# 21 of 24 later convolutions move from VectorE to TensorE, and the skip term from TensorE to ScalarE

## The chip, the cores and the metric

The kernel runs on one core of a Trainium2 chip. The metric is the device time of one execution in microseconds. Instructions are issued in program order on five engines, which wait for each other only through semaphores: TensorE (PE), VectorE (DVE), ScalarE (ACT), GpSimd (POOL) and SyncE (SP), which issues most of the transfers.

## The reference

For 2 x 1024 tokens with 512 features (all in float32) the reference computes a layer norm, a selective-scan block and a small top-2-of-8 mixture of experts, and joins them:

```
xn  = layernorm(x)
x, gate = split(xn @ W_in.T)                      # 1024 channels each
xc  = conv_b + sum_j conv_w[:, j] * xpad[:, j:j+L]   # 4 taps, causal, per channel
x   = silu(xc)
ts, B, C = rms(split(x @ W_x.T))                  # 32, 16, 16
dt  = softplus(ts @ W_dt.T + b_dt)
state = state * exp(dt * A) + (dt * x) * B        # 16 states per channel, over time
y   = (sum_n state * C + x * D) * silu(gate)
s   = y @ W_out.T
g   = silu(mixture of 2 of 8 experts on xn)
out = x_in + s * g
```

## The kernel before

The 2048 tokens are cut into four chunks c of 512 (two per batch row), and the 1024 channels into eight blocks t of 128. A tile n = 8c + t is one block of one chunk. Its 16 states are worked in four quads: quad m = 4n + q has four recurrences (r = 0 to 3) over 512 time steps, each with 32 channels x 4 states on the partitions. "Low" is r = 0, 1, "high" is r = 2, 3.

For each quad: POOL multiplies `rep` (dt * x, spread over partitions by a transfer through DRAM) with B into one of four ring buffers of `drive` (`drives`, L567). ACT writes the decays exp(dt * A) into the four banks of `sc_ps` (`decays`, L799), two banks at a time, each after DVE or POOL is done with them. DVE runs the recurrences (`scans`, L1174) and multiplies by C (`products`, L1184); in most tiles POOL multiplies the low half of three or four quads instead (`low_products`, L580). PE sums over the states into `y_ps` (`sums`, L1434), after a start value that `skip` puts there: a matmul of x with a diagonal matrix of D (L1428), whose diagonal ACT writes (`diagonal`, L852). At the end DVE multiplies `y_ps` by the gate (`gate_tile`, L1201), a quad later than the last scans of the tile, behind the first quad of the next.

During chunk c the eight blocks of x for chunk c + 1 are made, each in four steps. PE projects into the bank `x_ps` (`next_x`, `project_x`, L1329). ACT copies it, with three columns of the chunk before, to `x_pad` and writes the first tap with its bias back over `x_ps` (`copy_x`, L703 to L710). DVE adds the other three taps, one instruction each, the last into `xy` (`convolve`, L1113). ACT takes the SiLU (`silu_x`, L715). "Early" blocks (1, 3, 5, 7) are in tiles t = 3, 4, 5, 6 ahead of the high scans of quad 4n + 1, "late" blocks (0, 2, 4, 6) in tiles t = 2, 3, 4, 5 behind the high products of quad 4n + 2. There is one `x_ps` bank and one `x_pad`, so each block waits for the one before it.

In the same tile dt of tile n + 2 is made: a matmul (`step_sizes`), ACT's Abs, Exp and Ln (`softplus`), and three instructions and a product on DVE (L1153 to L1157, L1149). In nine tiles (`pe_log`) PE adds the four parts by matmuls with the identity instead (`add_log`, L1378 to L1381), one of them the maximum, which ACT writes to `t_r`. Two "slots" of 128 gathered tokens go through an expert per tile in the middle of each row: POOL issues the gather, PE turns the rows (`turn_slot`), ACT copies them (`copy_slot_T`), PE multiplies (`expert`), ACT copies the result out (`copy_slot_y`). SP loads the expert's 1024 KB for each, and the weights of the next projections.

The order on each engine is written out by hand in one loop over n per engine. No planner changes it.

Of the kernel before, what the change touches and what calls it, by code (L numbers as in the profile page):

```python
# [50 lines left out]
LATE_X = {2: 0, 3: 2, 4: 4, 5: 6}  # L51

# [47 lines left out]
def scan_moe(nc, x, wx_in, wg_in, wdt_in, wxp, wring, gate_w, means, a_log, conv_w, conv_b, d_skip,  # L100
             token_ids, route_consts, bc_dram, rep_rows, xn_rows, xnT_rows, order, slot_rows, s_rows, out):
    with ExitStack() as ctx:
# [47 lines left out]

        w_gate = t_r[:, 0:HK * CH].rearrange("p (k e) -> p k e", k=HK)
# [120 lines left out]
        diag_ok, skip_mm = sem("diag_ok"), sem("skip_mm")  # L272
        x_mm, x_ev = sem("x_mm"), sem("x_ev")
        pad_ok, tap_ok, halo_ok = sem("pad_ok"), sem("tap_ok"), sem("halo_ok")
# [32 lines left out]

        def drives_done(eng, count):
            eng.wait_ge(drive_ok, count)
# [6 lines left out]
        def _(sp):  # L316
# [125 lines left out]
            for n in range(TILES):  # L442
                c, t = divmod(n, NT)
                b, even = c // PER_ROW, c % PER_ROW == 0
                first_slot, second_slot = slots_at(c, t)
                if n == 2:
                    for half in range(2):
                        sp.dma_start(w_out[:, HK * half:HK * (half + 1), :], wring[E + half]).then_inc(s_wo, 16)
                chunk_end = t == NT - 1 and c < NCH - 1
                if not even and t == NT - 2:  # L450
                    load_kept(c - 1)
                    load_residual(c - 1)
                if c == NCH - 1 and t == NT - 2:
# [24 lines left out]
                if c and t == 1 and c + 1 < NCH:  # L478
                    load_xnT(c + 1)
                if first_slot is not None:  # L480
                    load_expert(b, first_slot + 2)
                if chunk_end:
                    spread_b(c + 1, NQ - 1)
                    spread_c(c + 1, 1)
                if late_x(c, t) is not None:
                    load_w_x(NT * (c + 1) + late_x(c, t) + 1)
                if early_x(c, t) == NT - 1 and c + 2 < NCH:
                    load_w_x(NT * (c + 2))
                if second_slot is not None:
                    load_expert(b, second_slot + 2)  # L490
                if not even and t == NT - 1:
# [187 lines left out]
        def _(act):  # L679
# [16 lines left out]
            def copy_x(j):  # L696
                c, t = divmod(j, NT)
                kept = j - 2 if j < NT else j
                if kept > 0:
                    act.wait_ge(conv_ok, kept)  # L700
                    act.wait_ge(halo_ok, kept)
# [10 lines left out]
            def silu_x(j):  # L712
                c, t = divmod(j, NT)
                act.wait_ge(conv_ok, j + 1)
                act.activation(xy[:, c % 2, t, :], xy[:, c % 2, t, :], ACT.Silu).then_inc(x_ok, 1)  # L715
# [24 lines left out]
            def exponent(k):  # L740
# [6 lines left out]
                if pe_log(k):  # L747
                    act.activation(t_r[:, :], dt_ps[:, :], ACT.Relu).then_inc(relu_ok, 1)
# [100 lines left out]
            def diagonal(n):  # L849
                if n:  # L850
                    act.wait_ge(skip_mm, n)
                act.activation(diag[:, :], ident[:, :], ACT.Copy, scale=dsk[:, n % NT:n % NT + 1]).then_inc(diag_ok, 1)  # L852
# [53 lines left out]
            for n in range(TILES):  # L906
# [19 lines left out]
                diagonal(n)  # L926
# [11 lines left out]
                decays(m + 1, 1)  # L938
                copy_slot_T(b, first_slot)
# [41 lines left out]
        def _(dve):  # L981
# [311 lines left out]
        def _(pe):  # L1293
# [39 lines left out]
            def next_x(j):  # L1333
                c, t = divmod(j, NT)
                pe.wait_ge(s_wx, 16 * (j - NT + 1))
                pe.wait_ge(conv_ok, j)
# [10 lines left out]
                project_x(j, lambda h: w_x[:, h, :])  # L1347

# [23 lines left out]
            def add_log(k):  # L1372
# [5 lines left out]
                pe.matmul(dt_ps[:, :], ident[:, :], t_e[:, :], start=True, stop=False)  # L1378
                pe.matmul(dt_ps[:, :], ident[:, :], t_w[:, :], start=False, stop=False)
                pe.matmul(dt_ps[:, :], ident[:, :], t_l[:, :], start=False, stop=False)  # L1380
                pe.matmul(dt_ps[:, :], ident[:, :], t_r[:, :], start=False, stop=True).then_inc(log_mm, 1)  # L1381
# [41 lines left out]
            def skip(n):  # L1423
                c, t = divmod(n, NT)
                pe.wait_ge(diag_ok, n + 1)
                if n:
                    pe.wait_ge(gated, n)
                pe.matmul(y_ps[:, :], diag[:, :], xy[:, c % 2, t, :], start=True, stop=False).then_inc(skip_mm, 1)  # L1428

            def sums(m):  # L1430
                low_done(pe, m)
                pe.wait_ge(high_ok, m + 1)
                for r in range(NR):
                    last = pe.matmul(y_ps[CH * r:CH * (r + 1), :], stack[:, :], drive[:, m % RING, r, :],  # L1434
                                     start=False, stop=(m % NQ == NQ - 1))
# [65 lines left out]
            for n in range(TILES):  # L1501
# [14 lines left out]
                turn_slot(b, first_slot)  # L1516
                skip(n)
# [4 lines left out]
                if rms_tile:  # L1522
                    pe.wait_ge(conv_ok, NT * (c + 2))
# [19 lines left out]
                expert(b, second_slot)  # L1543
# [4 lines left out]
                sums(m + 2)  # L1548
                if not even and t in (0, 1):
# [81 lines left out]
```

## Time and profile before

| | us |
|---|---|
| median of three timed runs | 1090.31 (1086.61 to 1090.49) |
| span of the profiled execution, first to last instruction | 1086.8 |
| busy in the span: DVE, POOL, PE, ACT | 1022.8, 926.3, 872.1, 733.8 |
| convolutions of chunks 1 to 3 on DVE | 24 |
| matmuls of `skip` on PE (records, two for each) | 64 |

For the profiled execution only the span is given; it is 3.5 us under the median and 0.2 over the fastest timed run. Where a row has the count of matmul records, two records are one float32 matmul here. The profile's idle time of an engine is put down to the one that released it last.

### The profile page before, as it was taken

To read this page: it belongs to the slowest core of one execution; us is meant where nothing else is said; L and a number is where in the kernel's file an instruction comes from. 1 tells how busy PE (TensorE), PEld (TensorE's weight loads), DVE (VectorE), ACT (ScalarE), POOL (GpSimd) and SP (SyncE) were. 2 spreads that over 40 slices of the span, in tenths; PEclk is the share of its full clock that TensorE was granted. 3 is DMA by queue.
4 is the path that set the end of the run, shared out by engine and by line. 5 is a ranking of instruction groups with operands and counts; after the bars stand their busy time and mean duration, and the time that the engine had idled before them with its cause. 6 is when DMAs were issued, how large, how long until landed. Compare 5 with 4: busy or idle time off the path is not lost.

```text
span 1086.8 us, 10255 instructions
## 1 busy us (share of the span) xinstructions
PE 872.1 (80%) x2774; PEld 323.8 (30%) x2774; DVE 1022.8 (94%) x1044; ACT 733.8 (68%) x1285; POOL 926.3 (85%) x365
## 2 busy tenths in 40 slices
PE   9944569798889998988656778989788997778576
PEld 5321123233223433333112223333223342223122
DVE  6779999999999999999999999899999999999998
ACT  3655567787787667766775667778767566676574
POOL 0629899999989889989889989798998978998995
PEclk9976788999989999999967879999999999799789
DMA  9355586556476665666743554766548566565714
GB/s 331 120 161 199 107 268 232 212 198 232 167 274 240 232 238 207 170 182 210 204 164 122 185 181 152 274 242 227 190 165 287 188 224 232 184 225 182 280 33 151
DMA packets 78089, 219.26 MB, mean 202 GB/s; under 512 B 15824, under 2 KB 17232, under 8 KB 71376
## 3 DMA queue, kind: packets, MB, share of 16 engines
q1 hardware_dynamic: 58096, 166.67, 44.7%
q10 hardware_dynamic: 12672, 31.46, 7.8%
q0 software_dynamic: 7264, 20.47, 6.9%
q8 instruction: 23, 0.38, 0.1%
q14 instruction: 34, 0.28, 0.1%
HBM read 176.85 MB, written 41.72 MB: 201 GB/s over the span
## 4 chain that ended last, share of the span: by engine, by line
DVE 36%; PE 22%; POOL 15%; issue 12%; DMA 9%; ACT 4%; SPq 2%; DVEq 0%; ACTq 0%; POOLq 0%
DVE sc_ps L1174 16%; POOL drive L567 10%; DVE drive L1174 6%; PE x_ps L1466 6%; DMA rep<-rep_rows 5%; DVE drive L1184 3%; PE f_ps L1419 3%; POOL drive L580 3%; PE y_ps L1434 3%; DMA x_slot<-xn_rows,slot_tok 2%; PE dt_ps L1394 2%; DVE x_ps L1113 2%; PE x_ps L1329 1%; PE x_ps L1351 1%; SPq L382 1%
## 5 line engine op out<-in xcount | busy, mean ns | idle before, releaser
L567 POOL TENSOR_TENSOR drive<-rep,b_all 128x2048 f32<-128x2048 f32 x127 | 575.8, 4538 | 44.1 <-DMA rep<-rep_rows 40.7
L799 ACT ACTIVATE sc_ps<-rep,a_neg 128x512 f32<-128x512 f32 x512 | 332.0, 681 | 86.2 <-DVE drive L1184 57.3
L1434 PE MATMUL y_ps<-drive,stack 128*32 128x512 f32 x1024 | 156.1, 687 | 89.7 <-DVE drive L1184 62.8
L1184 DVE TENSOR_TENSOR drive<-sc_ps,c_all 128x1024 f32<-128x1024 f32 x177 | 216.8, 1225 | 5.9
L1174 DVE TENSOR_TENSOR_SCAN sc_ps<-sc_ps,state,drive 128x512 f32<-128x512 f32 x178 | 218.4, 1273 | 3.8 <-ACT sc_ps L799 3.2
L1174 DVE TENSOR_TENSOR_SCAN sc_ps<-sc_ps,drive 128x512 f32<-128x512 f32 x176 | 205.3, 1212 | 5.5 <-ACT sc_ps L799 4.4
L580 POOL TENSOR_TENSOR drive<-drive,c_all 128x1024 f32<-128x1024 f32 x79 | 186.4, 2360 | 6.1 <-ACT state L778 6.1
L1419 PE MATMUL f_ps<-w_ring,xT_slot 128*128 128x512 f32 x368 | 176.5, 624 | 12.1 <-ACT xT_slot L811 12.1
L1394 PE MATMUL dt_ps<-xnT,w_g 128*128 128x512 f32 x232 | 117.8, 655 | 20.5 <-ACT dtu L766 20.4
L1419 PEld LDWEIGHTS f_ps<-w_ring,xT_slot 128*128 128x128 f32 x368 | 71.5, 201 | 118.3 <-issue 118.0
L1174 DVE TENSOR_TENSOR_SCAN drive<-sc_ps,state,drive 128x512 f32<-128x512 f32 x78 | 95.5, 1266 | 2.8 <-ACT sc_ps L799 2.8
L1174 DVE TENSOR_TENSOR_SCAN drive<-sc_ps,drive 128x512 f32<-128x512 f32 x80 | 93.1, 1205 | 0.0
L1329 PE MATMUL x_ps<-xnT,w_x 128*128 128x512 f32 x192 | 89.7, 611 | 2.7 <-DMA w_x<-wx_in 2.7
L1466 PE MATMUL x_ps<-w_out,xy 128*128 128x512 f32 x176 | 84.8, 629 | 0.0
L1434 PEld LDWEIGHTS y_ps<-drive,stack 128*32 128x32 f32 x1024 | 21.9, 114 | 183.8 <-issue 142.3
L1394 PEld LDWEIGHTS dt_ps<-xnT,w_g 128*128 128x128 f32 x232 | 46.0, 209 | 97.1 <-issue 97.1
L778 ACT ACTIVATE state<-sc_ps 128x2 f32<-128x2 f32 x88 | 14.9, 169 | 71.0 <-DVE drive L1184 70.3
L536 POOL DMA_INDIRECT x_slot<-xn_rows,slot_tok x46 | 45.5, 989 | 20.0 <-PE f_ps L1408 13.7
L1370 PE MATMUL dt_ps<-dt_in,w_dt 128*128 128x512 f32 x64 | 44.4, 783 | 14.2 <-DVE dt_in L1231 13.0
L1408 PE MATMUL f_ps<-ident,x_slot 128*128 128x128 f32 x184 | 29.4, 284 | 31.9 <-DMA x_slot<-xn_rows,slot_tok 26.8
L1428 PE MATMUL y_ps<-xy,diag 128*128 128x512 f32 x64 | 35.8, 643 | 20.7 <-DVE xy L1201 20.7
L1329 PEld LDWEIGHTS x_ps<-xnT,w_x 128*128 128x128 f32 x192 | 35.5, 193 | 56.3 <-issue 52.7
(200 smaller groups left out, 1093.8 us busy)
## 6 DMA issues: line engine op xcount, KB each, us to landing
rep<-rep_rows SPq DMA_DIRECT2D x128, 512.0 KB, 6.7
w_ring<-wring SPq DMA_DIRECT2D x46, 1024.0 KB, 5.6
rep_rows<-dtu ACTq DMA_DIRECT2D x32, 512.0 KB, 3.3
slot_rows<-y_slot ACTq DMA_DIRECT2D x46, 256.0 KB
w_g<-wg_in SPq DMA_DIRECT2D x32, 256.0 KB, 2.7
w_x<-wx_in SPq DMA_DIRECT2D x24, 256.0 KB
xn_rows<-rep SPq DMA_DIRECT2D x16, 256.0 KB, 2.2
b_all<-bc_rows SPq DMA_DIRECT2D x16, 256.0 KB, 4.3
```

Of the source, the lines that this page charges most:

```text
L536: pool.indirect_dma_start(x_slot[:, :], None, xn_rows[:, :], bass.IndirectOffsetOnAxis(ap=slot_tok[:, m:m + 1], axis=0)).then_inc(s_gx, 16)
L567: pool.tensor_tensor(drive[:, m % RING, :, :], rep[:, n % 2, :, 1, :], b_all[:, q:q + 1, :].broadcast_to([P, NR, TC]), ALU.mult).then_inc( ...
L580: pool.tensor_tensor(drive[:, m % RING, 0:2, :], drive[:, m % RING, 0:2, :], c_all[:, q:q + 1, :].broadcast_to([P, 2, TC]), ALU.mult).then ...
L799: act.activation(sc[:, r, :], rep[:, n % 2, r, 0, :], ACT.Exp, scale=a_neg[:, lo:lo + 1]).then_inc(decay_ok, 1)
L1174: dve.tensor_tensor_scan(to, sc[:, r, :], drive[:, m % RING, r, :], state[:, lo:lo + 1] if follows else 0.0, ALU.mult, ALU.add).then_inc(s ...
L1184: dve.tensor_tensor(drive[:, m % RING, 2 * h:2 * h + 2, :], sc[:, 2 * h:2 * h + 2, :], c_all[:, q:q + 1, :].broadcast_to([P, 2, TC]), ALU. ...
L1329: last = pe.matmul(x_bank(j), w(h), xnT[:, c % 2, h, :], start=(h == 0), stop=(h == HK - 1))
L1370: pe.matmul(dt_ps[:, :], w_dt[:, t, :], dt_in[:, :], start=True, stop=True).then_inc(dt_mm, 1)
L1394: mm = pe.matmul(gate_bank(c, t)[:, :], w_g[:, h, :], xnT[:, c % 2, h, :], start=(h == 0), stop=(h == HK - 1))
L1419: last = pe.matmul(f_ps[:, :], xT_slot[:, h, :], w_ring[:, j % 2, h, :], start=(h == 0), stop=(h == HK - 1))
L1434: last = pe.matmul(y_ps[CH * r:CH * (r + 1), :], stack[:, :], drive[:, m % RING, r, :], start=False, stop=(m % NQ == NQ - 1))
L1466: last = pe.matmul(bank, xy[:, c % 2, t, P * i:P * (i + 1)], w_out[:, t, :], start=(t == 0), stop=(t == NT - 1))
```

## The change

- In chunks 1 to 3 the blocks 0 to 6 get their last three taps on PE: three matmuls with diagonal matrices (`add_taps`), added to the first tap that ACT has written in `x_ps`. Block 7 and chunk 0 stay on DVE. The matrices (192 KB for a block) are loaded by SP (`load_taps`) into `t_r`.
- For early blocks ACT's SiLU reads `x_ps`. For late blocks ACT copies `x_ps` to `xy` first (`take_x`), behind the softplus, and the SiLU follows in the next tile as before.
- On PE the early taps stand before `skip`; `sums(m + 1)` moves ahead of the late projection; the late taps and the second expert stand behind `sums(m + 2)`. On ACT the late `copy_x` moves behind the decays of the low half of quad m + 3.
- From tile 1 on, `skip` is an ACT instruction that writes x * D into `y_ps`, and the sums are added to it. It stands behind the high decays of quad m + 1. The diagonal is left for tile 0.
- In `pe_log` tiles ACT writes the maximum over `dt_ps` in place, and PE adds three parts.

```diff
+PE_TAPS = (0, 1, 2, 3, 4, 5, 6)
+def pe_taps(j):
+    return j >= NT and j % NT in PE_TAPS
+def late_taps(j):
+    return pe_taps(j) and j % NT in LATE_X.values()
...
+        def x_bank_free(eng, j):
+            if late_taps(j - 1):
+                eng.wait_ge(x_took, took(j))
+            elif pe_taps(j - 1):
+                eng.wait_ge(x_ok, j)
+            else:
+                eng.wait_ge(conv_ok, dve_convs(j))
...
+            def load_taps(j):
+                if j is None or not pe_taps(j):
+                    return
+                if pe_convs(j):
+                    sp.wait_ge(taps_mm, pe_convs(j))
+                else:
+                    sp.wait_ge(lgT_mm, 1)
+                sp.dma_start(taps, taps_in[j % NT]).then_inc(s_tap, 16)
...
             def silu_x(j):
...
+                elif pe_taps(j):
+                    act.wait_ge(taps_mm, pe_convs(j + 1))
+                    xy_free(act, c)
+                    rows = x_ps[:, :]
...
+            def take_x(j):
+                if not late_taps(j):
+                    return
+                c, t = divmod(j, NT)
+                act.wait_ge(taps_mm, pe_convs(j + 1))
+                xy_free(act, c)
+                act.copy(xy[:, c % 2, t, :], x_ps[:, :]).then_inc(x_took, 1)
...
-                    act.activation(t_r[:, :], dt_ps[:, :], ACT.Relu).then_inc(relu_ok, 1)
+                    act.activation(dt_ps[:, :], dt_ps[:, :], ACT.Relu).then_inc(relu_ok, 1)
...
+            def skip(n):
+                if n == 0:
+                    return
+                c, t = divmod(n, NT)
+                act.wait_ge(gated, n)
+                act.activation(y_ps[:, :], xy[:, c % 2, t, :], ACT.Copy, scale=dsk[:, t:t + 1]).then_inc(skip_ok, 1)
...
                 decays(m + 1, 1)
+                skip(n)
                 copy_slot_T(b, first_slot)
...
                 copy_slot_y(b, first_slot)
+                store_slot(b, first_slot)
+                decays(m + 3, 0)
                 if late is not None:
                     copy_x(NT * (c + 1) + late)
-                store_slot(b, first_slot)
-                decays(m + 3, 0)
                 copy_slot_T(b, second_slot)
...
+                if late is not None:
+                    take_x(NT * (c + 1) + late)
...
+            def add_taps(j):
+                if not pe_taps(j):
+                    return
+                pe.wait_ge(s_tap, 16 * pe_convs(j + 1))
+                pe.wait_ge(tap_ok, j + 1)
+                for k in range(1, K):
+                    last = pe.matmul(x_ps[:, :], taps[:, k - 1, :], x_pad[:, k:k + TC], start=False, stop=(k == K - 1),
+                                     skip_group_check=True)
+                last.then_inc(taps_mm, 1)
...
                 turn_slot(b, first_slot)
+                if early_x(c, t) is not None:
+                    add_taps(NT * (c + 1) + early_x(c, t))
                 skip(n)
...
+                sums(m + 1)
                 if late is not None:
                     next_x(NT * (c + 1) + late)
                 turn_slot(b, second_slot)
-                sums(m + 1)
...
-                expert(b, second_slot)
+                if late is None:
+                    expert(b, second_slot)
...
                 sums(m + 2)
+                if late is not None:
+                    add_taps(NT * (c + 1) + late)
+                    expert(b, second_slot)
```

## Rows read from the trace of the kernel before

**Rows 1.** The page's busy line: us, share of the span, instructions.
```profile
PE 872.1 (80%) x2774; PEld 323.8 (30%) x2774; DVE 1022.8 (94%) x1044; ACT 733.8 (68%) x1285; POOL 926.3 (85%) x365
```

**Rows 2.** Windows of tiles 4 and 27: busy us by engine, granted clock, transfers.
```profile
212.00:241.00 29.00, 25.69 (x83) 9.40 (x83) 28.72 (x29) 23.96 (x47) 26.52 (x10) 1.00 0.60 207
930.00:959.00 29.00, 21.06 (x70) 7.38 (x68) 28.29 (x27) 18.65 (x29) 28.64 (x10) 0.88 0.61 205
```

**Rows 3.** Groups of instructions, whole span: busy us, mean ns of one, idle before.
```profile
L799 ACT ACTIVATE sc_ps<-rep,a_neg 128x512 f32<-128x512 f32 x512 | 332.0, 681 | 86.2 <-DVE drive L1184 57.3 <-DVE drive L1174 10.6 <-DMA rep<-rep_rows 6.4
L1329 PE MATMUL x_ps<-xnT,w_x 128*128 128x512 f32 x192 | 89.7, 611 | 2.7 <-DMA w_x<-wx_in 2.7
L1113 DVE SCALAR_TENSOR_TENSOR x_ps<-x_pad,cw,x_ps 128x512 f32<-128x512 f32 x54 | 40.4, 749 | 3.1 <-ACT x_ps L708 2.0 <-DVE moe L993 0.2
L1428 PE MATMUL y_ps<-xy,diag 128*128 128x512 f32 x64 | 35.8, 643 | 20.7 <-DVE xy L1201 20.7
L708 ACT ACTIVATE x_ps<-x_pad,cb,cw 128x512 f32<-128x512 f32 x27 | 21.1, 782 | 2.5
L705 ACT COPY x_pad<-x_ps 128x512 f32<-128x512 f32 x27 | 15.5, 575 | 16.6 <-PE x_ps L1329 16.6
L852 ACT ACTIVATE diag<-ident,dsk 128x128 f32<-128x128 f32 x32 | 13.0, 407 | 0.0
```

**Rows 4.** DVE in order of time, tiles 2 and 4: start, us, [idle before].
```profile
167.30 2.35 DVE L1174 TENSOR_TENSOR_SCAN sc_ps<-sc_ps,drive 128x512 f32<-128x512 f32 x2 [0.99 <-ACT sc_ps L799]
...
215.73 1.52 DVE L1113 SCALAR_TENSOR_TENSOR x_ps<-x_pad,cw,x_ps 128x512 f32<-128x512 f32 x2
...
217.95 2.34 DVE L1174 TENSOR_TENSOR_SCAN sc_ps<-sc_ps,drive 128x512 f32<-128x512 f32 x2
...
223.71 2.32 DVE L1174 TENSOR_TENSOR_SCAN sc_ps<-sc_ps,drive 128x512 f32<-128x512 f32 x2
...
235.19 2.33 DVE L1174 TENSOR_TENSOR_SCAN drive<-sc_ps,drive 128x512 f32<-128x512 f32 x2
```

**Rows 5.** ACT in order of time, tile 4.
```profile
211.73 0.78 ACT L708 ACTIVATE x_ps<-x_pad,cb,cw 128x512 f32<-128x512 f32 x1
...
215.84 0.20 ACT L778 ACTIVATE state<-drive 128x2 f32<-128x2 f32 x1 [0.82 <-DVE drive L1174]
...
221.84 1.30 ACT L799 ACTIVATE sc_ps<-rep,a_neg 128x512 f32<-128x512 f32 x2
...
232.17 1.30 ACT L799 ACTIVATE sc_ps<-rep,a_neg 128x512 f32<-128x512 f32 x2
```

**Rows 6.** PE in order of time, tiles 2 and 4.
```profile
164.73 1.12 PE L1408 MATMUL f_ps<-ident,x_slot 128*128 128x128 f32 x4 [5.84 <-DMA x_slot<-xn_rows,slot_tok]
...
215.17 3.67 PE L1419 MATMUL f_ps<-w_ring,xT_slot 128*128 128x512 f32 x8 [0.36 <-ACT xT_slot L811]
...
239.18 1.07 PE L1434 MATMUL y_ps<-drive,stack 128*32 128x512 f32 x8
```

**Rows 7.** The page's transfers: count, KB each, median us to landing.
```profile
w_ring<-wring SPq DMA_DIRECT2D x46, 1024.0 KB, 5.6
```

**Rows 8.** POOL in order of time, tile 4.
```profile
222.87 4.54 POOL L567 TENSOR_TENSOR drive<-rep,b_all 128x2048 f32<-128x2048 f32 x1 [2.12 <-DMA rep<-rep_rows]
```

**Rows 9.** DVE in order of time: the gates that end tiles 1, 5, 9, 13, 25, 29.
```profile
148.31 0.68 DVE L1201 TENSOR_TENSOR xy<-y_ps,gate 128x512 f32<-128x512 f32 x1
...
273.64 0.68 DVE L1201 TENSOR_TENSOR xy<-y_ps,gate 128x512 f32<-128x512 f32 x1
...
390.85 0.69 DVE L1201 TENSOR_TENSOR xy<-y_ps,gate 128x512 f32<-128x512 f32 x1 [0.56 <-PE y_ps L1434]
...
519.84 0.68 DVE L1201 TENSOR_TENSOR xy<-y_ps,gate 128x512 f32<-128x512 f32 x1
...
900.50 0.69 DVE L1201 TENSOR_TENSOR xy<-y_ps,gate 128x512 f32<-128x512 f32 x1 [0.99 <-PE y_ps L1434]
...
1015.92 0.68 DVE L1201 TENSOR_TENSOR xy<-y_ps,gate 128x512 f32<-128x512 f32 x1
```

More of the change, by code:

```diff
@@ L51, with pe_convs, dve_convs, took @@
 LATE_X = {2: 0, 3: 2, 4: 4, 5: 6}
+PE_TAPS = (0, 1, 2, 3, 4, 5, 6)
+def pe_taps(j):
+    return j >= NT and j % NT in PE_TAPS
+def pe_convs(k):
+    return sum(pe_taps(j) for j in range(k))
+def dve_convs(k):
+    return k - pe_convs(k)
+def late_taps(j):
+    return pe_taps(j) and j % NT in LATE_X.values()
+def took(k):
+    return sum(late_taps(j) for j in range(k))
 def act_turns(k):
@@ L149, in scan_moe @@
         slot_tok = sb("slot_tok", BATCH * SLOTS, dtype=I32)
+        taps = t_r[:, 0:(K - 1) * P].rearrange("p (k e) -> p k e", k=K - 1)
         w_gate = t_r[:, 0:HK * CH].rearrange("p (k e) -> p k e", k=HK)
@@ L481, in _ @@
                     load_expert(b, first_slot + 2)
+                if late_x(c, t) is not None and t > 2:
+                    load_taps(NT * (c + 1) + late_x(c, t))
                 if chunk_end:
@@ L490, in _ @@
                     load_expert(b, second_slot + 2)
+                if t == 1 and c < NCH - 1:
+                    load_taps(NT * (c + 1) + late_x(c, t + 1))
+                if early_x(c, t + 1) is not None:
+                    load_taps(NT * (c + 1) + early_x(c, t + 1))
                 if not even and t == NT - 1:
@@ L699, in copy_x @@
                 if kept > 0:
-                    act.wait_ge(conv_ok, kept)
+                    if pe_taps(kept - 1):
+                        act.wait_ge(taps_mm, pe_convs(kept))
+                    else:
+                        act.wait_ge(conv_ok, dve_convs(kept))
                     act.wait_ge(halo_ok, kept)
@@ L713, in silu_x @@
                 c, t = divmod(j, NT)
-                act.wait_ge(conv_ok, j + 1)
-                act.activation(xy[:, c % 2, t, :], xy[:, c % 2, t, :], ACT.Silu).then_inc(x_ok, 1)
+                if late_taps(j):
+                    act.wait_ge(x_took, took(j + 1))
+                    rows = xy[:, c % 2, t, :]
+                elif pe_taps(j):
+                    act.wait_ge(taps_mm, pe_convs(j + 1))
+                    xy_free(act, c)
+                    rows = x_ps[:, :]
+                else:
+                    act.wait_ge(conv_ok, dve_convs(j + 1))
+                    rows = xy[:, c % 2, t, :]
+                act.activation(xy[:, c % 2, t, :], rows, ACT.Silu).then_inc(x_ok, 1)
+            def take_x(j):
[5 more added lines that the diff above has]
+                act.copy(xy[:, c % 2, t, :], x_ps[:, :]).then_inc(x_took, 1)
             act.wait_ge(ln_v, 1)
@@ L1377, in add_log @@
                 pe.wait_ge(relu_ok, pe_logs(k + 1))
[L1378 to L1381, printed above, removed]
+                pe.matmul(dt_ps[:, :], ident[:, :], t_e[:, :], start=False, stop=False, skip_group_check=True)
+                pe.matmul(dt_ps[:, :], ident[:, :], t_w[:, :], start=False, stop=False, skip_group_check=True)
+                pe.matmul(dt_ps[:, :], ident[:, :], t_l[:, :], start=False, stop=True, skip_group_check=True).then_inc(log_mm, 1)
             def gate_in(n):
@@ L1423, in skip @@
             def skip(n):
-                c, t = divmod(n, NT)
-                pe.wait_ge(diag_ok, n + 1)
                 if n:
-                    pe.wait_ge(gated, n)
-                pe.matmul(y_ps[:, :], diag[:, :], xy[:, c % 2, t, :], start=True, stop=False).then_inc(skip_mm, 1)
+                    pe.wait_ge(skip_ok, n)
+                    return
+                pe.wait_ge(diag_ok, 1)
+                pe.matmul(y_ps[:, :], diag[:, :], xy[:, 0, 0, :], start=True, stop=False)
             def sums(m):
@@ L1434, in sums @@
                     last = pe.matmul(y_ps[CH * r:CH * (r + 1), :], stack[:, :], drive[:, m % RING, r, :],
-                                     start=False, stop=(m % NQ == NQ - 1))
+                                     start=False, stop=(m % NQ == NQ - 1), skip_group_check=m >= NQ)
                 last.then_inc(sum_ok, 1)
@@ L1590 @@
     gate_w[:, :E] = v["gate_w"]
+    taps = np.zeros((NT, P, K - 1, P), f)
+    for k in range(1, K):
+        taps[:, np.arange(P), k - 1, np.arange(P)] = v["conv_w"].reshape(NT, P, K)[:, :, k]
     consts = np.ones((P, CONSTS), f)
@@ L1607 @@
         "gate_w": gate_w.reshape(HK, P, CH).transpose(1, 0, 2),
+        "taps_in": taps,
         "means": mean_w,
```

33 lines of the change are left out of this document (19 added, 14 removed).

## The prediction

> **What bounds the kernel now.** I read the page's busy line first: VectorE (DVE) is busy 94% of the span, GpSimd (POOL) 85%, TensorE (PE) 80%, ScalarE (ACT) 68% [rows 1]. The start-up is in these shares. Then I read windows of single tiles, for how close the others are: in the 29 us of tile 4 DVE works 28.72, POOL 26.52, PE 25.69, ACT 23.96 [rows 2]. So DVE sets the pace, with three engines close behind. All four are coupled: ACT writes the decays into the four banks of `sc_ps` only when DVE has left them, DVE scans only behind them, and PE must finish `sums(m)` before POOL refills the ring. A saving on DVE is therefore worth what the next engine lets through.
>
> **What is removed from DVE.** 21 convolutions of three instructions. One takes 749 ns [rows 3]; on the clock the three stand between the scan pair that ends at 215.73 and the next at 217.95, so 2.22 us each [rows 4]. 21 x 2.22 = 46.6 us, all of it on the engine that sets the pace. That is the largest possible gain: a span of 1040.2.
>
> **What it is replaced by.** Chunks 1 to 3 take nine of these convolutions as early ones (before the scans of the tile's second quad, t = 3, 4, 5) and twelve as late ones (t = 2 to 5). I walk through tile 4, which has one of each, and move every piece by what changed ahead of it.
>
> *Early.* After low(m+1) DVE goes straight to the scans at 215.73. The next half quads follow without a gap, so DVE stands at the scans of (m+2, high) at 223.71 - 2.22 = 221.49 [rows 4]. ACT writes those decays at 221.84, one of them takes 0.68, so the first is there at 222.52 [rows 3, 5]. It can't come sooner: ahead of it on ACT lie two table loads, two SiLUs and the gate's SiLU without a gap. The skip activation of ScalarE is new ahead of this, but ACT stood idle 0.82 us at 215.84 for DVE [rows 5]. The skip is priced between the decay's 681 ns (ScalarE, SBUF to PSUM) and the 782 of the scaled first tap (the same way) [rows 3]; I take 0.68, and 0.82 covers both ends. Without that cover it would delay the decays by 0.7 per tile. Stall 1.03, net gain 2.22 - 1.03 = 1.2 per early convolution: 9 x 1.2 = 10.8.
>
> *Late.* DVE comes to low(m+4) at 235.19 now [rows 4]; less 1.2 and 2.22 it would be 231.8. ACT starts those decays at 232.17 [rows 5], gets `take_x` in front (a 128x512 copy out of PSUM, 575 ns by the copy to x_pad [rows 3]), so 232.75, and the first is ready at 233.4. Stall 1.6, net 0.6. This holds where softplus n+2 ends on PE. Where it ends on DVE, three instructions of about 0.7 and the product stand before low(m+4) and cover it, and only some 0.2 is lost before the decays of (m+3, high): net 2.0. Of the nine late ones in t = 3 to 5, five are of the first kind (n = 4, 11, 12, 13, 20), four of the second: 5 x 0.6 + 4 x 2.0 = 11.0. At t = 2 (three tiles) another thing sets the pace: in tile 2 PE waits 5.84 us for the gathered rows at 164.73 [rows 6], ACT's `copy_slot_T` stands behind it, and DVE waits 0.99 for the decays behind that [rows 4]. There a convolution less is only a longer wait, between 0 and 2.2; I take 0.7, since only tile 2's row shows it: 2.1.
>
> *PE.* A matmul pair of `project_x` costs 89.7/96 = 0.93 us of busy time, one skip pair 35.8/32 = 1.1 [rows 3]. A tile with two tapped projections gets 6 x 0.93 = 5.6 more and 1.1 less: 25.69 + 4.5 = 30.2 busy in tile 4 [rows 2], more than the 27.4 that this tile would take by the sums above. Busy records overlap, so this isn't a hard bound, but PE has no slack left in t = 3 to 5. The early taps cost little: they need ACT's first tap, written at 211.73 + 0.78 = 212.5 [rows 5], and until the expert's matmuls start at 215.17 PE has only the skip and idle time [rows 6]; 3 x 0.93 ends at about 215.3, and the skip that went to ACT comes at the same time. So `sums(m)` moves by 0.6 at most. The late taps and the second expert go behind `sums(m+2)`, and with the next projection push `sums(m+3)` from 239.18 [rows 6] to about 239.3, while DVE has come forward by 1.8. In tile 5 PE then starts as late as before, its projection for the late convolution ends later relative to DVE, and `copy_x` on ACT (in order ahead of the decays of (m+3, high)) waits for it. My walk through tile 5 gives 2.2 saved where the terms above give 3.2; bounds are 0 and a whole late saving of 2. I charge 1.0 in t = 4 and t = 5 of chunks 0 and 2, half in chunk 1 (longer tiles): -5.
>
> *The rest.* `add_log` loses one matmul (nine times) and the maximum goes in place: no DVE instruction changes, and the later steps of t wait for ACT's Ln, so 0 (bounds: 0.93 us gained or lost in each of nine tiles, if it stood on the path). 31 diagonals of 407 ns are replaced by 31 skips: +0.27 us each on ACT [rows 3], hidden by its waits; `skip` waits for `gated`, which DVE gives one instruction after the product that releases the decays ahead of it, so it waits for nothing new; behind it stand `copy_slot_T`, and through that PE's expert and `sums(m)`. The new loads are 21 x 192 KB on SP's queue. The tightest is the late one, issued behind an expert load of 1024 KB, which itself waits for the expert matmuls (end 215.17 + 3.67 = 218.8 [rows 6]). With 5.6 us to landing [rows 7] and 192 KB more at the same rate (1.1) it is there at 225.5; PE wants it at about 226.9, when the late first tap ends, which now follows the decays of (m+3, low). Cost 0, with 1 us as the upper bound in nine tiles. SP's waits for `taps_mm` follow waits for the expert's matmuls that now end later than the taps, so they hold up nothing more, and the rep loads keep their release, `gate_in`'s last matmul.
>
> **Sum.** 10.8 + 11.0 + 2.1 - 5 = 18.9, say 19 to 20. POOL must allow it: it starts drive(4n+4) at 222.87, after 2.12 idle for the rep rows [rows 8], and is done 7.8 us before DVE wants it at 235.19 [rows 4]; 5 us stay. The span is 1086.8, and the median of the timed runs 1090.31 is 3.5 above it, which I carry along: 1090.3 - 20 = **1070**.
>
> By the Trainium skill (Perfetto Trace Analysis, Identifying the Most-Contended Engine) TensorE's matmul busy share is no measure of how near it is to its limit, since matmuls are pipelined; then the 30.2 above would be no bound and the 5 us charged to PE would fall away, which would give 1065. Rows 2 can't settle it, since they are of the busy kind; the other sentences keep the charge.
>
> **Rivals.**
> (a) *The gap closes further.* Chunk 3 has no convolutions: tiles 26 to 29 run from 900.50 to 1015.92, 28.9 us each, against 31.3 in tiles 2 to 5 (148.31 to 273.64) and 32.2 in tiles 10 to 13 (390.85 to 519.84) [rows 9]. If the tapped tiles came down to 28.9: 4 x 2.4 + 4 x 3.3 and chunk 2 like chunk 0, so 10 + 13 + 10 = 33, or 1057. For it: the late `copy_x` goes behind the decays of (m+3, low) on ACT, which takes pressure from one of its three tight places. Against: chunk 3 has no projection, no first tap and no state to keep on ACT (18.65 of 29 busy against 23.96), and even so POOL is at 28.64 of 29 there [rows 2], so this is about the floor that POOL sets. The whole 46.6 would give 1044; the same skill section tells to work on the most-occupied engine, which would be DVE. Chance 0.25 for (a), of which 0.04 for the whole.
> (b) *PE becomes the bound, slower.* The place is `next_x`(late) in t = 3 to 5, held up on PE by its new wait for `silu_x` of the early tile, and by taps; ACT stands in `copy_x`, DVE waits for decays. If PE needs its 30.2 busy us and keeps the 3.3 of idle time it has in tile 4 (29 - 25.69) [rows 2], a tile takes 33.5 against the 31.3 of tiles 2 to 5 [rows 9]: 9 x 2.2 = 20 lost, 1110. It decides as soon as PE's idle time in such a tile stays above 31.3 - 30.2 = 1.1 us. Against it: most of that idle time is just where the early taps go. Chance 0.11.
> (c) *Nothing moves.* The stalls at (m+2, high) and low(m+4) grow by all that is taken away, because ACT's sequence is full, and taps or gathers arrive late: 1090. For it: ACT's 0.58 and PE's 4.5 more in each tapped tile, and tile 2's wait. Against: t = 3 and t = 5 have the cover of DVE's three softplus steps. Chance 0.09.
>
> **How the numbers follow.** Forecast 0.55 (its own range 1062 to 1080), (a) 0.25, (b) 0.11, (c) 0.09. Half a per cent is 5.5 us, what a measurement of this kernel can tell: faster is forecast and (a), 0.80; same 0.09; slower 0.11. The range reaches down to between (a) and the whole, 1050, and up to (c), 1090.
>
> **What would show it.** Right: DVE's busy time falls by about 47 us while its idle time grows by about 27 (46.6 - 20), with new waits `sc_ps` scan <- ACT decays in t = 3 to 5, after (m+2, high) and at low(m+4) of tiles 4, 12 and 20; PE's busy time is up by some 16 us (21 x 2.8 less 31 x 1.1 and 9 x 0.93) and PE's idle before the expert's matmuls in tile 4 shrinks; POOL's durations unchanged. The PE step is wrong if the scans never wait for `copy_x`. Wrong altogether if DVE's idle time grows by over 40 us, or if tiles 6, 7 and those of chunk 3, which have no tapped convolution, get longer: then the skip on ACT isn't hidden.

## The result, and the profile after

The changed kernel takes 1143.91 us (median; 1141.73 to 1146.49), the kernel before 1089.35 on the same chip: a ratio of 1.050, 95% interval 1.0475 to 1.0524. It is slower by 55 us where 20 us of gain were forecast, and outside the range. The profiled execution has a span of 1141.6, 54.8 more than before.

The page's busy line of the changed kernel:
```profile
PE 898.6 (79%) x2820; PEld 338.1 (30%) x2820; DVE 980.9 (86%) x981; ACT 747.8 (66%) x1297; POOL 925.9 (81%) x365
```
Against [rows 1] DVE has lost 41.9 us of busy time, as intended, and idles 160.7 instead of 64.0: 96.7 more. Nobody else has much more to do (PE 26.5, ACT 14.0, POOL nothing). So this is waiting, and the waits say for what (who waited for whom: us, times, longest):
```profile
PE y_ps L1524 <- POOL drive L634: 85.3, 39, 6.8
DVE sc_ps L1255 <- ACT sc_ps L873: 62.3, 31, 5.1
...
POOL x_slot L590 <- PE f_ps L1498: 49.0, 16, 5.5
ACT x_pad L762 <- PE x_ps L1410: 48.4, 20, 6.0
ACT xT_slot L885 <- PE f_ps L1498: 45.1, 24, 4.4
...
ACT xy L789 <- PE x_ps L1436: 38.0, 11, 7.5
...
DVE drive L1255 <- ACT sc_ps L873: 34.4, 13, 5.6
```
PE's wait in `sums` for POOL's low product was 26.9 us before (15 times, 5.3 at the longest):
```profile
PE y_ps L1434 <- POOL drive L580: 26.9, 15, 5.3
```

The time from gate to gate by tile, worked out from the starts of `gate_tile`, shows where it is lost (us):

| tiles | before | after |
|---|---|---|
| t = 2 to 5 of chunks 0 to 2 (12 tiles) | 380.2 | 428.0 |
| the other tiles 1 to 23 (11) | 339.8 | 344.0 |
| chunk 3 (8) | 232.4 | 236.0 |

All but 8 us of it lies in the tapped tiles. Tile 4 went from 28.6 to 36.7. Its window, against the first of [rows 2] (DVE 28.72 of 29):
```profile
224.00:261.00 37.00, 33.35 (x108) 13.13 (x100) 24.52 (x23) 25.75 (x51) 28.59 (x11) 0.95 0.58 209
```
DVE stops three times for decays and once for dt, where [rows 4] have no such stop in tile 4 (DVE in order of time):
```profile
236.04 2.35 DVE L1255 TENSOR_TENSOR_SCAN sc_ps<-sc_ps,drive 128x512 f32<-128x512 f32 x2 [2.54 <-ACT sc_ps L873]
...
244.63 2.35 DVE L1255 TENSOR_TENSOR_SCAN sc_ps<-sc_ps,drive 128x512 f32<-128x512 f32 x2 [2.74 <-ACT sc_ps L873]
...
252.57 2.34 DVE L1255 TENSOR_TENSOR_SCAN drive<-sc_ps,drive 128x512 f32<-128x512 f32 x2 [4.33 <-ACT sc_ps L873]
257.06 0.69 DVE L1230 TENSOR_TENSOR dtu<-dt_ps,xy 128x512 f32<-128x512 f32 x1 [2.16 <-PE dt_ps L1471]
```
PE in the same tile. Before, the last sums of this tile at 239.18 [rows 6] had no wait, nor had the three ahead of them; now two of the sums wait for POOL:
```profile
237.01 1.07 PE L1524 MATMUL y_ps<-drive,stack 128*32 128x512 f32 x8 [1.18 <-POOL drive L634]
238.01 3.70 PE L1410 MATMUL x_ps<-xnT,w_x 128*128 128x512 f32 x8
...
245.48 1.07 PE L1524 MATMUL y_ps<-drive,stack 128*32 128x512 f32 x8 [2.48 <-POOL drive L634]
246.47 4.54 PE L1436 MATMUL x_ps<-x_pad,t_r 128*128 128x512 f32 x6
250.85 3.59 PE L1509 MATMUL f_ps<-w_ring,xT_slot 128*128 128x512 f32 x8
254.28 1.02 PE L1469 MATMUL dt_ps<-t_e,ident 128*128 128x512 f32 x2
```
And ACT, with the two copies that wait for PE and have the decays behind them:
```profile
241.74 0.58 ACT L762 COPY x_pad<-x_ps 128x512 f32<-128x512 f32 x1 [2.54 <-PE x_ps L1410]
...
251.05 0.58 ACT L789 COPY xy<-x_ps 128x512 f32<-128x512 f32 x1 [2.60 <-PE x_ps L1436]
```
Read together (the experiments below test it): POOL finishes a low product late, PE stands in the sum over it, the projection, the taps, the expert and the logarithm stand behind that sum, ACT stands in a copy for them, DVE in a scan for ACT. It closes to a loop on POOL, which issues the next gather only after PE has turned the rows (POOL in order of time):
```profile
229.10 0.99 POOL L590 DMA_INDIRECT x_slot<-xn_rows,slot_tok  x1 [4.62 <-PE f_ps L1498]
```

### The profile page after: what moved, and what is told of

The parts are those of the page before. It is cut to its first block, busy times and chain, and to the rows that moved or that the text cites. A ratio compares the mean times of both kernels' runs of the same rounds, so it can differ in the third digit from the quotient of the medians.

```text
span 1141.6 us, 10307 instructions
## 1 busy us (share of the span) xinstructions
PE 898.6 (79%) x2820; PEld 338.1 (30%) x2820; DVE 980.9 (86%) x981; ACT 747.8 (66%) x1297; POOL 925.9 (81%) x365
## 4 chain that ended last, share of the span: by engine, by line
PE 36%; POOL 20%; DMA 18%; DVE 15%; issue 5%; SPq 4%; ACT 2%; DVEq 0%; POOLq 0%; ACTq 0%
DMA rep<-rep_rows 13%; POOL drive L621 12%; DVE sc_ps L1255 7%; PE f_ps L1509 6%; PE dt_ps L1484 6%; PE x_ps L1556 5%; PE y_ps L1524 5%; POOL drive L634 4%; PE x_ps L1436 4%; PE x_ps L1410 4%; SPq L430 3%; DMA rep_rows<-dtu 2%; DVE drive L1265 2%; DMA slot_rows<-y_slot 1%; PE x_ps L1442 1%
## 5 line engine op out<-in xcount | busy, mean ns | idle before, releaser
L1524 PE MATMUL y_ps<-drive,stack 128*32 128x512 f32 x1024 | 160.2, 703 | 161.4 <-POOL drive L634 85.3
L1509 PE MATMUL f_ps<-w_ring,xT_slot 128*128 128x512 f32 x368 | 174.2, 618 | 18.4 <-ACT xT_slot L885 18.4
L1484 PE MATMUL dt_ps<-xnT,w_g 128*128 128x512 f32 x232 | 120.1, 666 | 20.9 <-ACT dtu L840 18.9
L1410 PE MATMUL x_ps<-xnT,w_x 128*128 128x512 f32 x192 | 92.0, 624 | 0.0
L1556 PE MATMUL x_ps<-w_out,xy 128*128 128x512 f32 x176 | 85.3, 632 | 0.0
L1484 PEld LDWEIGHTS dt_ps<-xnT,w_g 128*128 128x128 f32 x232 | 46.6, 212 | 97.3 <-issue 97.3
L1436 PE MATMUL x_ps<-x_pad,t_r 128*128 128x512 f32 x126 | 68.7, 687 | 0.0
L885 ACT COPY xT_slot<-f_ps 128x512 f32<-128x512 f32 x46 | 26.6, 578 | 45.4 <-PE f_ps L1498 45.1
L1461 PE MATMUL dt_ps<-dt_in,w_dt 128*128 128x512 f32 x64 | 40.4, 718 | 14.2 <-DVE dt_in L1312 13.0
L1556 PEld LDWEIGHTS x_ps<-w_out,xy 128*128 128x128 f32 x176 | 33.7, 200 | 50.3 <-issue 49.7
```

What stands on the lines that cost most here:

```text
L1410: last = pe.matmul(x_bank(j), w(h), xnT[:, c % 2, h, :], start=(h == 0), stop=(h == HK - 1))
L1436: last = pe.matmul(x_ps[:, :], taps[:, k - 1, :], x_pad[:, k:k + TC], start=False, stop=(k == K - 1), skip_group_check=True)
L1484: mm = pe.matmul(gate_bank(c, t)[:, :], w_g[:, h, :], xnT[:, c % 2, h, :], start=(h == 0), stop=(h == HK - 1))
L1509: last = pe.matmul(f_ps[:, :], xT_slot[:, h, :], w_ring[:, j % 2, h, :], start=(h == 0), stop=(h == HK - 1))
L1556: last = pe.matmul(bank, xy[:, c % 2, t, P * i:P * (i + 1)], w_out[:, t, :], start=(t == 0), stop=(t == NT - 1))
```

## The experiments

Every ratio is to runs of the kernel before on the same chip, whose median went from 1087.95 to 1090.79; "median, ratio [95% interval]". Two kernels leave two of the three tap matmuls out.

**First: is it the taps?** Four versions of the changed kernel.

No block tapped:
```diff
-PE_TAPS = (0, 1, 2, 3, 4, 5, 6)
+PE_TAPS = ()
```


> No block is tapped on TensorE (PE_TAPS is empty): all 24 convolutions are back on VectorE, while the skip on ScalarE, the maximum in place and the new order of the sums, of the late projection, of copy_x and of the second expert stay. Theory W (TensorE's work sets the length of a tapped tile): 1085 to 1090, since PE has 43 us less work than before. Theory C (the late taps stand behind the third sums and take_x ahead of the decays): also 1085 to 1092. Theory S (the skip on ScalarE and the new order cost the time, not the taps): 1120 to 1144.

Measured: 1136.33, 1.040 [1.033, 1.048]. Theories W and C are both out as the cause of the loss: with 24 convolutions on DVE and none on PE, 46 of the 55 us are still lost (S had 1120 to 1144). Something else in the change costs it.

Only the early blocks (`PE_TAPS = (1, 3, 5)`):

> Only the nine early blocks (1, 3, 5) are tapped on TensorE; the twelve late ones are back on VectorE, so take_x is gone. Theory W: a loss in proportion to TensorE's added work, 9 of 21 of it, so about 1089 + 23 = 1112. Theory C: the early taps fill idle time and save VectorE about 1 us each, 1080 to 1090.

Measured: 1132.13, 1.040 [1.034, 1.046]. In neither range.

Only the late blocks (`PE_TAPS = (0, 2, 4, 6)`):

> Only the twelve late blocks (0, 2, 4, 6) are tapped on TensorE; the nine early ones are on VectorE. Theory W: 12 of 21 of the loss, about 1120. Theory C: nearly all of the loss, 1135 to 1145.

Measured: 1138.65, 1.044 [1.037, 1.051]. Inside C's range, but without meaning once the first is known.

All blocks, one matmul instead of three:
```diff
-                for k in range(1, K):
+                for k in range(K - 1, K):
```


> All 21 blocks as in the changed kernel, but TensorE multiplies only the last tap of each and leaves out the two others: 42 matmuls of 0.86 us less, every wait and every other instruction stays. Theory W: 36 us less, about 1108. Theory C: the late taps end 1.7 us sooner and the wait of take_x shrinks by that in twelve tiles, 20 us at most, 1122 to 1135; the wait for the third sums stays.

Measured: 1123.56, 1.030 [1.024, 1.035]. By the medians some 20 us for 36 us of matmuls: in C's range and far from W's, but C was already out as the cause.

**Second: the order on PE.** In the kernel without taps DVE waited 8.7 us for a late first tap in tile 2, that for `next_x`, and that stood behind `sums(m + 1)`. So the kernel *before* got this one edit, and nothing else:
```diff
+                sums(m + 1)
                 if late is not None:
                     next_x(NT * (c + 1) + late)
                 turn_slot(b, second_slot)
-                sums(m + 1)
```


> The kernel before with one edit: on TensorE sums(m + 1) moves ahead of the late projection and the second slot's transposes. Theory O (this order alone costs the time: PE stands in sums(m + 1) for POOL's low product, next_x and copy_x stand behind it, and the late first tap comes late): 1115 to 1140, with VectorE waiting for the late convolution. Rival E (what costs is the second expert behind sums(m + 2), or the skip on ScalarE): 1086 to 1093.

Measured: 1141.92, 1.050 [1.047, 1.052], 2 us above O's range. One moved call with no instruction added loses 52 us, about as much as the whole change. PE and then DVE in tile 2:
```profile
163.61 1.93 PE L1434 MATMUL y_ps<-drive,stack 128*32 128x512 f32 x8 [8.30 <-POOL drive L580]
165.47 5.11 PE L1329 MATMUL x_ps<-xnT,w_x 128*128 128x512 f32 x8
```
```profile
172.11 1.55 DVE L1113 SCALAR_TENSOR_TENSOR x_ps<-x_pad,cw,x_ps 128x512 f32<-128x512 f32 x2 [11.51 <-ACT x_ps L708]
```
PE waits 8.30 us for a product that POOL reaches only after a drive and a gather. The projection that stood ahead of these sums in program order filled such time; now, behind them, it comes 10 us later than in the kernel before (155.19 there, by the same view), it runs partly at half clock (5.11 us for what takes 3.70), and DVE waits 11.51. Over the whole kernel DVE's wait for a first tap grew from 2.0 us to
```profile
DVE x_ps L1113 <- ACT x_ps L708: 50.3, 13, 11.5
```
and the profiled span by 44.3: the late first taps account for the loss.

The same move taken out of the changed kernel, in three versions (no taps, all, early only):

> The changed kernel without taps on TensorE (all 24 convolutions on VectorE), with sums(m + 1) back behind the late projection and the transposes; skip on ScalarE, maximum in place, copy_x behind the decays, second expert behind sums(m + 2) stay. Theory O: 1080 to 1095, the 45 us of the kernel without taps are gone. Rival E: stays at 1115 to 1137.

> The changed kernel with all 21 blocks tapped on TensorE and sums(m + 1) back behind the late projection and the transposes. Theory O with room on PE: 1070 to 1085, the gain that was forecast. Rival W (TensorE's work, some 32 us per tapped tile, is a second bound under the order's): 1095 to 1125. Rival E: no change, 1135 to 1144.

> As the last, but only the nine early blocks are tapped on TensorE. Theory O: 1075 to 1085 (nine early savings of 1.2 us each). Rival W: 1090 to 1105, since the tapped tiles t = 3 to 5 have 2.6 us more for PE each. Rival E: 1115 to 1132.

Measured: 1120.20, 1.026 [1.022, 1.031]; 1150.17, 1.054 [1.048, 1.059]; 1117.49, 1.028 [1.023, 1.032]. The first and the last lie in E's ranges, the one with all taps above all three. Theory O holds for the edit alone and falls as the only cause: with all taps this move alone gives nothing back (1.054 against 1.050). Without taps, 16 us came back, not 45, and DVE now waited 3.0 to 8.5 us for `dt_ps <- PE` in six tiles: 4, 11, 12, 13, 18, 20, the late tiles whose logarithm is on PE.

**Third: the second expert.** Again the kernel *before* with one edit:
```diff
-                expert(b, second_slot)
+                if late is None:
+                    expert(b, second_slot)
...
                 sums(m + 2)
+                if late is not None:
+                    expert(b, second_slot)
```


> The kernel before with one edit: in the tiles with a late block the second expert stands behind sums(m + 2) on TensorE. Theory Q (PE stands in the sum for POOL's low product and the expert and the logarithm's matmuls behind it come late): 1105 to 1125, with VectorE waiting for dt_ps in tiles 4, 11, 12, 13, 18, 20. Rival (it costs only together with the skip on ScalarE): 1088 to 1095.

Measured: 1121.45, 1.030 [1.027, 1.034], in Q's range. PE and then DVE in tile 4:
```profile
236.20 1.93 PE L1434 MATMUL y_ps<-drive,stack 128*32 128x512 f32 x8 [5.66 <-POOL drive L580]
238.06 5.67 PE L1419 MATMUL f_ps<-w_ring,xT_slot 128*128 128x512 f32 x8
```
```profile
247.20 0.69 DVE L1149 TENSOR_TENSOR dtu<-dt_ps,xy 128x512 f32<-128x512 f32 x1 [5.63 <-PE dt_ps L1381]
```
DVE waits for `dt_ps` like this in tiles 4, 11, 12, 13, 18 and 20, as forecast: 4.7 to 6.5 us each, 33.0 together, and the loss is 33.

Then the changed kernel with both moves undone:
```diff
-                sums(m + 1)
                 if late is not None:
                     next_x(NT * (c + 1) + late)
                 turn_slot(b, second_slot)
+                sums(m + 1)
...
-                if late is None:
-                    expert(b, second_slot)
+                expert(b, second_slot)
...
                 sums(m + 2)
                 if late is not None:
                     add_taps(NT * (c + 1) + late)
-                    expert(b, second_slot)
```
without taps, with all, with the early ones only, and with all but the late taps ahead of the third sums:

> No taps on TensorE, and both of PE's moves undone: sums(m + 1) behind the late projection and the transposes, the second expert ahead of sums(m + 2). What stays of the change is the skip on ScalarE, the maximum in place and copy_x behind the decays. Theory Q (PE, in program order, stands in a sum for POOL's low product, and what was moved behind it is late; each of the two moves alone is enough to cost 30 to 50 us): 1083 to 1093. Rival S (the skip on ScalarE costs): stays near 1110 to 1120.

> All 21 blocks tapped on TensorE with both moves of PE undone; the late taps stand behind sums(m + 2), take_x waits for them. Theory Q: the late taps are the third thing behind a sum that waits for POOL, with take_x and the decays of the next tile behind them, so 1110 to 1140. Rival W (PE's work alone): 1095 to 1110, whatever the place of the taps.

> Both moves of PE undone and only the nine early blocks tapped on TensorE; the twelve late ones are on VectorE. Theory Q: the early taps lie in PE's idle time: 1073 to 1086, faster than before. Rival W: 1095 to 1105.

The last one, against the one with all taps:
```diff
+                if late is not None:
+                    add_taps(NT * (c + 1) + late)
                 sums(m + 2)
-                if late is not None:
-                    add_taps(NT * (c + 1) + late)
```


> As the last, but the late taps stand ahead of sums(m + 2), behind the second expert. Theory Q: nothing of the late block stands behind a sum that waits for POOL: 1070 to 1095. Rival W: the same as the last kernel, within 5 us.

Measured: no taps 1097.28, 1.0075 [1.005, 1.010]; all, behind the third sums, 1102.26, 1.010 [1.004, 1.016]; early only 1099.52, 1.010 [1.006, 1.015]; all, late ones ahead, 1086.50, 0.998 [0.994, 1.001]. 39 of the 46 us without taps are back. The late taps' place is worth 16 us (1102.26 to 1086.50), the same in kind. Q's ranges held only for the last one. No taps came out 4 us above its range, and the other two fell between 1095 and 1110, where rival W had them: Q had the cost of the late taps behind the sum too high and the early taps' gain too high. W in turn is out by the last one, which has all of PE's work and is 16 us faster. These four ran on one chip, so the taps themselves can be priced: from no taps to all taps in their best place here 11 us, and for the early nine alone nothing (1097.28 to 1099.52, intervals overlap). PE's wait for POOL over these kernels (in order: only the sums moved; only the expert moved; both undone without taps; the last one):
```profile
PE y_ps L1434 <- POOL drive L580: 53.0, 18, 8.3
```
```profile
PE y_ps L1434 <- POOL drive L580: 83.3, 22, 7.2
```
```profile
PE y_ps L1524 <- POOL drive L634: 25.5, 14, 4.9
```
```profile
PE y_ps L1524 <- POOL drive L634: 24.3, 16, 5.2
```
Over all kernels it is 19 to 33 us in those of 1103 us or less and 53 to 98 in those of 1117 or more. The size doesn't order the losses (53.0 goes with 1142, 83.3 with 1121): what counts is what stands behind the sum.

**Fourth: why then no gain?** With the late taps ahead of the third sums, DVE stood 3.52 us in tile 4 for the decays of (m + 4, low). ACT shows why:
```profile
236.91 0.59 ACT L789 COPY xy<-x_ps 128x512 f32<-128x512 f32 x1 [1.78 <-PE x_ps L1436]
237.39 0.21 ACT L852 ACTIVATE state<-drive 128x2 f32<-128x2 f32 x1
237.63 1.30 ACT L873 ACTIVATE sc_ps<-rep,a_neg 128x512 f32<-128x512 f32 x2
```
Three single edits to that kernel. `take_x` behind the decays:
```diff
-                if late is not None:
-                    take_x(NT * (c + 1) + late)
                 decays(m + 4, 0)
+                if late is not None:
+                    take_x(NT * (c + 1) + late)
```


> The kernel with both moves undone and the late taps ahead of sums(m + 2), with one more edit: on ScalarE take_x stands behind the decays of (m + 4, low), not ahead of them. If the 3.5 us that VectorE waits at low(m + 4) in tiles 4, 11, 13 and 20 are take_x's wait for the taps: 1068 to 1080. If the SiLU block at (m + 2, high) and PE's work are what is left: 1082 to 1090.

Measured: 1082.30, 0.995 [0.993, 0.997]. The wait in tile 4 fell to 1.14, but the next one, for `dt_ps`, took 2.30. The kernel is faster than before by a measurable half per cent, and in the second range, not the first. What this edit gave by itself (4 us by the medians, on another chip, with overlapping intervals) isn't clear of noise.

The late `copy_x` in its old place, ahead of the decays of (m + 3, low):

> The same kernel with the late taps ahead of sums(m + 2), take_x as in the changed kernel, and the late copy_x back ahead of the decays of (m + 3, low). If ScalarE's late first tap is what the taps wait for, they and take_x end about 1.3 us sooner: 1075 to 1085. If nothing waits there: 1084 to 1089. If the decays of (m + 3, low) become late: 1090 to 1100.

Measured: 1095.73, 1.009 [1.006, 1.012], in the third range. The new place is worth 9 us by the medians and 12 by the ratios: a part of the change that helps.

The skip back on PE:

> The same kernel with the skip back on TensorE (diagonal by ScalarE, start matmul behind the gate). If the skip on ScalarE is what leaves 7 us in the kernel without taps: 1075 to 1083. If PE's 0.9 us per tile in the tapped tiles count for more: 1088 to 1105. If neither: 1084 to 1089.

Measured: 1088.77, 1.001 [0.999, 1.004], in the last range. The skip on ACT is not a cost here; a gain of 2 to 4 us (0.998 against 1.001) is within the noise. What costs 7 us in the kernel without taps stays open.

**Fifth: what binds the mended kernel?** PE in tile 5 of the kernel with `take_x` behind (from one gate projection to the next, no idle time):
```profile
243.71 3.70 PE L1484 MATMUL dt_ps<-xnT,w_g 128*128 128x512 f32 x8
247.25 0.60 PE L1498 MATMUL f_ps<-ident,x_slot 128*128 128x128 f32 x4
247.69 2.74 PE L1436 MATMUL x_ps<-x_pad,t_r 128*128 128x512 f32 x6
250.27 3.59 PE L1509 MATMUL f_ps<-w_ring,xT_slot 128*128 128x512 f32 x8
253.79 1.06 PE L1524 MATMUL y_ps<-drive,stack 128*32 128x512 f32 x8
...
271.54 1.07 PE L1524 MATMUL y_ps<-drive,stack 128*32 128x512 f32 x8
272.54 1.98 PE L1484 MATMUL dt_ps<-xnT,w_g 128*128 128x512 f32 x4
```
Two kernels from there. Six logarithms back to DVE, two of three tap matmuls left out (the edit as above):
```diff
-VECTOR_LOG = (0, 1, 2, 3, 4, 5, 7, 8, 10, 11, 12, 16, 17, 18, 19, 21, 23, 24, 26, 27, 28, 29, 31)
+VECTOR_LOG = (0, 1, 2, 3, 4, 5, 6, 7, 8, 10, 11, 12, 13, 14, 15, 16, 17, 18, 19, 20, 21, 22, 23, 24, 26, 27, 28, 29, 31)
```


> The kernel with both moves of PE undone, the late taps ahead of sums(m + 2) and take_x behind the decays of (m + 4, low), and with softplus n = 6, 13, 14, 15, 20, 22 ending on VectorE as in the other tiles, not by three matmuls on TensorE. PE had no idle time in tiles 4 and 5 of the kernel it starts from (31.4 us from gate_in to gate_in in tile 4, 28.8 in tile 5). Theory W2 (with the order mended, PE's work is the bound in tapped tiles, and 2.6 us of it leave six of them): 1065 to 1076. Rival (ScalarE's SiLU block ahead of (m + 2, high) is the bound): 1079 to 1085, since VectorE gets 2.1 us of work back in these six tiles.

> The same starting kernel, but TensorE multiplies only the last tap of each block and leaves out the two others: 42 matmuls, 36 us of PE's time, less; every wait and all of VectorE's and ScalarE's work stay. Theory W2: 1055 to 1068, as what binds next is POOL at 28 to 29 us per tile. Rival (ScalarE's SiLU block): 1076 to 1083.

Measured: 1077.20, 0.988 [0.986, 0.990]; 1074.72, 0.988 [0.985, 0.992]. Both miss W2's ranges by a little (1 and 7 us) and both lie below the ScalarE range, the second nearer to it (1 us) than to W2's. PE's work counts, but 36 us less of it bring some 8. From gate to gate, tiles 4 and 20, where the logarithm was on PE, went from 29.9 to 28.2 and 27.7; tiles 13 and 18, where it was too, got no shorter (31.4 and 29.9; then 31.8 and 33.4, and 31.4 and 32.0). So PE's work is shown as the bound in some of these tiles only. Tile 5, which has no logarithm on PE, stayed at 30.29 with a third of the tap matmuls. There DVE stands at the end of a chain through PE and ACT. DVE in tile 5 of that kernel, then ACT:
```profile
250.74 2.34 DVE L1255 TENSOR_TENSOR_SCAN sc_ps<-sc_ps,drive 128x512 f32<-128x512 f32 x2 [2.54 <-ACT sc_ps L873]
```
```profile
243.56 0.58 ACT L885 COPY xT_slot<-f_ps 128x512 f32<-128x512 f32 x1 [0.91 <-PE f_ps L1498]
244.04 0.21 ACT L852 ACTIVATE state<-drive 128x2 f32<-128x2 f32 x1
244.28 1.30 ACT L873 ACTIVATE sc_ps<-rep,a_neg 128x512 f32<-128x512 f32 x2
245.60 1.28 ACT L1022 ACT_TABLE_LOAD   x1
...
248.51 1.28 ACT L1030 ACT_TABLE_LOAD   x1
...
250.01 1.30 ACT L873 ACTIVATE sc_ps<-rep,a_neg 128x512 f32<-128x512 f32 x2
```
PE turns the slot's rows (ends 243.5), ACT copies them, writes the low decays, goes through its SiLU block without a gap, and writes the high decays that DVE waits for. Whether this chain can be shortened by another order wasn't tried.

The first of these two is the best kernel of the study that computes everything: 1.2% faster than before. It has every convolution that was to move on PE, PE's old order, late taps ahead of the third sums, `take_x` behind the decays, and the dt of these six tiles on DVE. The last edit wasn't tried on the kernel before, so how much of the 1.2% it would give there, without any taps on PE, isn't known.

## Why the prediction was wrong, step by step

**The gain on DVE.** 46.6 us of time, by 2.22 per convolution. The busy time fell by 41.9 (2.0 each; the rest is the gap to the next scan). The step stands.

**The prices.** The skip on ACT was taken at 0.68 and measures 0.671, hidden as forecast outside the tapped tiles: tiles 26 to 29 have 114.6 us against 115.4 of [rows 9]. PE's busy time was to grow by some 16 us and grew by 26.5; the taps took 68.7 for 63 matmuls, 1.09 each and not 0.93, since part of them ran at a lower granted clock (0.66 from 246 to 249 us, where six records in tile 4 took 4.54 us; 2.74 in tile 5 of the kernel with `take_x` behind, called the mended kernel from here on).

**The step that failed** is "The late taps and the second expert go behind `sums(m+2)`, and with the next projection push `sums(m+3)` from 239.18 to about 239.3". The walk let PE pass `sums(m+1)` and `sums(m+2)` when DVE's *high* product was ready and never asked when POOL's *low* product was. It is the other half of the same wait, and over the kernel it went from 26.9 to 85.3 us. Alone in the old kernel, the move of `sums(m+1)`, which the prediction doesn't even mention, costs 52 us, and the move of the expert, which it took as 0.1 us of delay, costs 33. Together and with the taps they cost 55, not their sum. With all taps on PE, undoing the first alone gave nothing back (1150) and undoing both gave 48 us more (1102), as if either were enough to lengthen one loop; that is argued, and the expert's move undone alone wasn't run. In the sum the order changes had no term at all: every microsecond was spent on the new instructions.

**PE's work.** It was read from a window (25.69 of 29) and raised to 30.2. The window cut the tile badly: `gate_in` of tile 4 began ahead of it (PE, kernel before):
```profile
207.99 3.67 PE L1394 MATMUL dt_ps<-xnT,w_g 128*128 128x512 f32 x8 [2.04 <-ACT dtu L766]
```
From there to the next `gate_in` (240.18) are 32.2 us with 3.3 of idle time: 28.9 of work. In the mended kernel tile 4 takes 31.4 from `gate_in` to `gate_in` (212.31 to 243.71) without a gap, and tile 5 28.8. So PE had no room for two taps and a logarithm in a tile of 27.4. The Trainium skill (Perfetto Trace Analysis, Identifying the Most-Contended Engine) holds that PE's matmul busy share is no good measure of how near it is to its limit. In this case a record's duration overstates what a matmul takes (0.59 us a record, 0.43 between starts), but a stretch without gaps, from start to start, measures it, and it did bind in tiles 4 and 20. The same section says to optimize the most-occupied engine first. That was DVE, and of the 46.6 us taken off it the taps gave back 11 with PE's old order; with the new one the kernel lost 55.

**The stalls that were forecast** came where they were put, only larger: (m+2, high) was to be 1.03 and was 2.54, low(m+4) 1.6 and was 4.33 in tile 4. In the mended kernel they are 1.08 and 1.14 (tile 4). But tile 4 doesn't stand for the others: there the stall at (m+2, high) is 1.1 in tiles 4 and 20 and 2.5 to 3.2 in tiles 3, 5, 19 and 21, more than the 2.22 that an early convolution frees. So the term "9 x 1.2 = 10.8" was mis-sized too: with PE's old order the nine early taps alone gained nothing, and the step to all 21 gained 13, where the late terms had 11.0 + 2.1. Forecast (c) had the right kind and (b) the right victims (`next_x`, `copy_x`, then the decays), for a wrong reason: what (b) named was PE's work and the new wait for `silu_x`, what happened was a sum's old wait in a new place. (b) had 0.11.

**The signs to watch for** read as follows: DVE's idle time grew by 96.7, over the 40 that was set as "wrong altogether"; scans do wait behind `copy_x`; chunk 3 is unchanged but for tile 24 (34.4 against 30.8). Tiles 6 and 22 are longer by 1.8 each, which was a sign against the skip on ACT, but with PE's old order and the late taps ahead, the skip still on ACT, both are 0.4 to 0.6 shorter than before. So the skip is hidden, and it is the orders that lengthened them.

**What stays open**: 7 us of the kernel with no taps and the old order (the maximum in place, and the late `copy_x` with a convolution behind it, weren't tried apart), and how much of the mended kernel's rest is POOL (27.5 and 27.0 of 30 us busy in tiles 4 and 5, and 29.4 and 29.5 with the six logarithms back on DVE).

## What to carry to other kernels

When an instruction is moved on an in-order engine, list every semaphore of what it is now behind, with the time at which each is given, POOL's included; a wait that costs nothing while filler stands in front of it can delay all that is put behind it by its whole length. Measure an engine's need per iteration from one issue of an instruction to its next issue, minus the idle time between, not by a window at round numbers, and walk through one tile of each kind, not one tile for all. If a change has moves and new work in it, run the moves alone first: here one moved call reproduced 52 of the 55 us.

## What the runs showed of the hardware

ACT can write the start value of an accumulation in PSUM (x * D, 671 ns for 128x512) and PE's matmuls add to it, and the same with the first tap and the maximum. Of the skip no cost shows in tiles 26 to 29 (114.6 us against 115.4). A wait cost PE twice here. Windows of the kernel with only the sums moved (start:end, us, busy time and count of PE, PE's weight loads, DVE, ACT, POOL, then PE's granted clock, the DMA share, GB/s):
```profile
160.00:164.00 4.00, 0.39 (x4) 0.20 (x8) 0.60 (x1) 0.00 (x0) 4.00 (x3) 0.50 0.75 66
164.00:168.00 4.00, 4.00 (x11) 1.18 (x4) 0.00 (x0) 0.00 (x0) 4.00 (x1) 0.50 0.87 229
168.00:171.00 3.00, 3.00 (x11) 1.57 (x10) 0.00 (x0) 0.38 (x1) 0.02 (x1) 0.94 0.13 55
```
PE stood for 8.30 us before 163.61. The granted clock was 0.50 (the 1.2 GHz level) from 160 to 168, also over the first 4 us in which PE worked without a gap, and 0.94 after. So the eight records of the next projection took 5.11 us in place of 3.70.
